# The last group's rows of the first two experts by one-hot products instead of through the expert buffer

## The reference, cut to what matters

```
Q, K, V = sign(x * bq), sign(x * bk), x * bv
x1 = layernorm(x + where(causal, sigmoid(4 * Q @ K.T / sqrt(d)), 0) @ V)
probs = softmax(x1 @ w_router);  top1 = argmax(probs);  gate = probs[top1]
pos = cumsum(onehot(top1)) - 1;  accepted = pos < C
slot = where(accepted, top1 * C + pos, E * C)
buf = zeros(E * C + 1, H).at[slot].set(x1)
y = (silu(buf @ w_gate) * (buf @ w_up)) @ w_down      # for each expert
out = layernorm(x1 + where(accepted, y[slot] * gate, 0))
```

## Time and profile before

| | us |
|---|---|
| median of 3 runs | 535.84 (534.91 to 535.91) |
| the profiled execution | 535.45 |
| its span, first to last instruction | 533.7 |
| last product of attention starts | 300.09 |
| first product of expert 0 starts | 324.26 |
| PE busy over the span | 512.2 (96%) |

### The profile page before, as it was taken

One profiled execution on the slowest core, in us unless ns is written; L12 is line 12 of the kernel. 1 busy time (PEld: TensorE's weight loads), 2 busy tenths in 40 slices (PEclk: granted clock), 3 DMA queues, 4 the chain that ended last, 5 costly groups with the idle time before them and its releaser, 6 DMA issues.

```text
span 533.7 us, 12148 instructions
## 1 busy us (share of the span) xinstructions
PE 512.2 (96%) x3983; PEld 457.7 (86%) x4021; DVE 406.8 (76%) x1033; ACT 380.5 (71%) x774; POOL 383.8 (72%) x494
## 2 busy tenths in 40 slices
PE   6999999999999999999999988999999999999992
PEld 5889899898998898998989747999998999999991
DVE  3885888886777948798766636888888888888884
ACT  5886968878868869788686513677776766777763
POOL 4647878777879688777785270577787877788876
PEclk9999999999999999999999999999999999999997
DMA  8996332263332432318841016477776666777211
GB/s 249 367 360 198 90 100 61 80 178 102 110 85 82 123 110 80 92 50 276 246 158 62 2 43 160 120 235 220 207 230 205 200 194 207 207 238 216 77 42 51
DMA packets 91919, 81.54 MB, mean 153 GB/s; under 512 B 31642, under 2 KB 83082, under 8 KB 91856
## 3 DMA queue, kind: packets, MB, share of 16 engines
q1 hardware_dynamic: 84320, 66.38, 42.0%
q0 software_dynamic: 6912, 14.30, 7.7%
q10 hardware_dynamic: 624, 0.07, 0.1%
HBM read 44.33 MB, written 37.90 MB: 154 GB/s over the span
## 4 chain that ended last, share of the span: by engine, by line
PE 90%; issue 3%; POOL 2%; DMA 2%; DVE 2%; ACT 1%; SPq 0%; POOLq 0%; DVEq 0%
PE ps L937 12%; PE ps L938 12%; PE ps L939 12%; PE ps L915 11%; PE ps L1101 8%; PE ps L1109 7%; PE ps L1102 7%; PE ps L1137 5%; PE ps L1145 3%; PE ps L1074 3%; PE ps L956 2%; PE ps L969 2%; PE ps L1134 1%; PE ps L1136 1%; PE ps L1135 1%
## 5 line engine op out<-in xcount | busy, mean ns | idle before, releaser
L937 PE MATMUL ps<-v_hl,hl_ring 128*128 128x256 f32 x544 | 178.2, 328 | 0.2 <-DVE hl_ring L1217 0.2
L938 PE MATMUL ps<-v_hl,hl_ring 128*128 128x256 f32 x544 | 153.4, 282 | 0.0
L939 PE MATMUL ps<-v_hl,hl_ring 128*128 128x256 f32 x544 | 153.2, 282 | 0.0
L937 PEld LDWEIGHTS ps<-v_hl,hl_ring 128*128 128x128 f32 x544 | 103.4, 190 | 14.8 <-issue 0.6
L1217 DVE TENSOR_TENSOR hl_ring<-ps,hl_ring 128x512 fp32r<-128x512 f32 (+3 forms) x160 | 94.0, 601 | 18.7 <-ACT ps L710 13.2
L938 PEld LDWEIGHTS ps<-v_hl,hl_ring 128*128 128x128 f32 x544 | 103.5, 190 | 2.8
L708 ACT ACTIVATE hl_ring<-ps 128x512 fp32r<-128x512 f32 (+3 forms) x160 | 86.6, 541 | 23.2 <-PE ps L915 22.8
L939 PEld LDWEIGHTS ps<-v_hl,hl_ring 128*128 128x128 f32 x544 | 103.1, 190 | 0.0
L710 ACT ACTIVATE ps<-ps 128x512 f32<-128x512 f32 (+3 forms) x160 | 87.8, 548 | 0.0
L544 POOL DMA_INDIRECT expert_rows<-xrow,slot x64 | 64.4, 1006 | 29.3 <-issue 21.3
L1101 PE MATMUL ps<-hl_ring,v_hl 128*128 128x320 f32 x256 | 80.8, 328 | 0.3 <-DVE hl_ring L1488 0.3
(11 more groups left out here) (179 smaller groups left out, 1126.4 us busy)
## 6 DMA issues: line engine op xcount, KB each, us to landing
expert_rows<-xs SPq DMA_DIRECT2D x40, 258.0 KB, 6.6
xs<-expert_rows SPq DMA_DIRECT2D x32, 258.0 KB, 2.8
out_dram<-alone SPq DMA_DIRECT2D x16, 512.0 KB, 3.2
xall<-in_L_ffn_w_gate_dram SPq DMA_DIRECT2D x32, 256.0 KB, 4.1
xall<-in_L_ffn_w_up_dram SPq DMA_DIRECT2D x32, 256.0 KB, 4.3
xall<-in_L_ffn_w_down_dram SPq DMA_DIRECT2D x32, 256.0 KB, 4.9
xall<-in_L_attn_x_dram SPq DMA_DIRECT2D x15, 512.0 KB, 5.8
xs<-expert_rows SPq DMA_DIRECT2D x31, 64.5 KB, 3.2
```

Of the source, the lines that this page charges most:

```text
L937: mm(o, ah, v_hl[:, 0, j, :], start=(j == 0 and i % 2 == 0), stop=False, skip_group_check=True)
L938: mm(o, ah, v_hl[:, 1, j, :], start=False, stop=False, skip_group_check=True)
L939: last = mm(o, al, v_hl[:, 0, j, :], start=False, stop=(j == GT * g + i), skip_group_check=True)
```

## The change

Expert 0's and expert 1's rows are put together in two parts. After the scatter of `last + 2` has landed, SP loads the rows as they then are (`base_in`), with the last group's rows still zero; PE turns them with ordinary products with the identity that leave the accumulation open (`early_rows`). Once the slots of the last group are known, DVE compares them with the numbers of the slots of each expert (`slot_of`, written by POOL after the first sequence; `slot_f`, the slots as float) and writes tables of ones and zeros (`hits_0` 4 times 128x384, `hits_1` 4 times 128x256). PE adds the last group's rows times these tables into the same PSUM banks (`last_rows`), with the rows split into a high part by ACT (`last_h`) and a low part by POOL (`last_l`). The scatter of `last + 3` still takes place, behind the `base_in` waits, and the rows of experts 0 and 1 are loaded again, since gate, token numbers and residual are read from them.

Moved besides: `place` and `gate` of `last + 2` from behind the last attention step into steps 35 to 37; three of its four scatter transfers ahead of the last group's roots and the fourth between the two halves of them (`first_root`, `second_root`); the weight splits of experts 0 and 1 into attention (on ACT two steps earlier; the low part of expert 0 on DVE in step 33, that of expert 1 on POOL); the turned rows of expert 1 ahead of the products of expert 0, so that the first two turns of the expert stage lie in another order. The 49 `keep_warm` products and the two ahead of `turn(0, 0)` are gone.

```
+            pool.wait_ge(gate_step, 3 * (last + 2) + 2)
+            pool.wait_ge(wh_ready, 2)
+            g_.tensor_tensor(w_l[:, 1, :, :], raw[:, 1, 0:WK, :], w_h[:, 1, :, :].bitcast(F32), ALU.subtract)...
+            scatter(last + 2, 0, range(GT - 1))
+            first_root(last + 3)
+            scatter(last + 2, 0, range(GT - 1, GT))
+            second_root(last + 3)
             pool.wait_ge(x1_ready, x1_by_act(last + 3, GT))
             pool.wait_ge(x1_late, GT // 2)
+            pool.wait_ge(last_high, 1)
+            g_.tensor_tensor(last_l, xrow[:, 1, :, 0:D], last_h.bitcast(F32), ALU.subtract).then_inc(last_low, 1)
             token_numbers(last + 3, 1)
+            pool.wait_ge(base_in[0], 48)
+            pool.wait_ge(base_in[1], 16)
             scatter(last + 3, 1)
...
+            def early_rows(e):
+                pe.wait_ge(base_in[e], 48 if e == 0 else 16)
+                for c in range(DC):
+                    for t in range(CT if e == 0 else CFULL):
+                        mm(turned_tile(e, t, c), xs[:, e, t, c * P:(c + 1) * P], ident[:, :],
+                           start=(t == 0 and (e == 0 or c == 0)), stop=False, skip_group_check=True)
+            def last_rows(e, hits):
+                for i in range(GT):
+                    pe.wait_ge(hit_ready, e * GT + i + 1)
+                    for rows in (last_h, last_l):
+                        for c in range(DC):
+                            o = ps[:, c, 0:W0] if e == 0 else ps[:, M1, c * W1:(c + 1) * W1]
+                            last = mm(o, rows[:, i, c * P:(c + 1) * P], hits[:, i, :], start=False,
+                                      stop=(i == GT - 1 and rows is last_l), skip_group_check=True)
+                last.then_inc(xs_turned, 1)
+            early_rows(0)
+            early_rows(1)
+            pe.wait_ge(last_high, 1)
+            pe.wait_ge(last_low, 1)
+            last_rows(0, hits_0)
+            last_rows(1, hits_1)
+            turn(0, 0, ahead=False)
+            gate_up(0, 1, 0)
+            down(0, 0)
+            turn_x(0, 2)
+            gate_up(0, 1, 1)
...
+            for hits, at, w in ((hits_0, 0, W0), (hits_1, W0, W1)):
+                for i in range(GT):
+                    v_.tensor_scalar(hits[:, i, :], slot_of[:, at:at + w], slot_f[:, i:i + 1], None, ALU.is_equal)
```

More of the change, by code:

```diff
@@ L151, in bass_postln_attn_moe_kernel @@
                     for n in range(2))
+        last_h, last_l = (r_flat[:, n * 2 * XN + XN:n * 2 * XN + XN + GT * D].rearrange("p (i d) -> p i d", d=D)
+                          for n in range(2))
+        W0, W1 = CFULL * P + P, CFULL * P
+        hits_0, hits_1 = (v_hl[:, n, 2 * WK:2 * WK + w * GT // D, :].rearrange("p k f -> p (k f)")
+                          .rearrange("p (i t) -> p i t", t=w) for n, w in enumerate((W0, W1)))
         HN = FC * CAP
@@ L233, in bass_postln_attn_moe_kernel @@
         scattered = [sem(f"scattered{i}") for i in range(2)]
+        cols_ready = sem("cols_ready")
+        slots_known = sem("slots_known")
+        hit_ready = sem("hit_ready")
+        last_high = sem("last_high")
+        last_low = sem("last_low")
+        base_in = [sem(f"base_in{i}") for i in range(2)]
         raw_in = [sem(f"raw_in{i}") for i in range(UR)]
@@ L421, in _ @@
                 store_alone(last + q, q % 2)
-            for par in range(2):
-                sp.wait_ge(scattered[par], 16 * GT * B * NG // 2)
+            sp.wait_ge(scattered[0], 16 * GT * B * NG // 2)
+            sp.wait_ge(scattered[1], 16 * GT * (B * NG // 2 - 1))
+            for e in range(2):
+                if e == 1:
+                    sp.wait_ge(x1_ready, x1_by_act(last + NG - 1, GT))
+                    sp.wait_ge(x1_late, GT // 2)
+                sp.dma_start(xs[:, e, 0:CFULL, :], buf_rows[e * CAP:e * CAP + CFULL * P, :]
+                             .rearrange("(i p) w -> p i w", p=P)).then_inc(base_in[e], 16)
+                if e == 0:
+                    for h in range(2):
+                        sp.dma_start(xs[h * CREST:(h + 1) * CREST, 0, CFULL, :],
+                                     buf_rows[h * CAP + CFULL * P:(h + 1) * CAP, :]).then_inc(base_in[0], 16)
+            sp.wait_ge(scattered[1], 16 * GT * B * NG // 2)
+            load_xs(2)
+            sp.wait_ge(xs_turned, 2)
             load_xs(0)
-            sp.dma_start(xs[CREST:2 * CREST, 0, CFULL, :], buf_rows[CAP + CFULL * P:2 * CAP, :]).then_inc(rest_in[0], 16)
+            load_rest(1)
+            store_alone(last + NG - 1, (NG - 1) % 2)
+            load_xs(3)
             load_xs(1)
[L427 to L430, removed]
+            load_ids(0)
+            load_rest(0)
+            load_ids(1)
             load_rest(2)
             load_rest(3)
-            for e in range(U):
+            for e in range(2, U):
                 load_ids(e)
@@ L537, in token_numbers, with scatter @@
                 atleast(pool, tok_step, G * 2 + 2, settle=True)
-            def scatter(G, par):
+            def scatter(G, par, tiles=range(GT)):
                 atleast(pool, gate_ready, G + 1, settle=True)
                 atleast(pool, slot_ready, G + 1, settle=True)
-                for i in range(GT):
+                for i in tiles:
                     g_.indirect_dma_start(
@@ L750, in batch @@
                     weights(b, k)
+                    if last and k == NS - 6:
+                        act.wait_ge(pv_done, (B - 1) * NS + OFF[3] + WK)
+                        high_weights(0, 0)
                     for g in (3, 0, 1, 2):
@@ L776, in batch @@
                             values_high(bb, q)
[L777 removed]
+                    if last and k == NS - 4:
                         act.wait_ge(pv_done, (B - 1) * NS + OFF[3] + 2 * WK)
[L780 removed]
+                        high_weights(0, 1)
             for tiles, landed, done in ((slice(0, GT // 2), x_half, sgn_half), (slice(GT // 2, GT), x_in[0], sgn_ready)):
@@ L800, in _ @@
             copy_x1t(B * NG - 1, range(1))
+            act.wait_ge(x1_late, GT // 2)
+            s_.activation(last_h, xrow[:, 1, :, 0:D], ACT.Copy).then_inc(last_high, 1)
             copy_lgt(B * NG - 1)
@@ L855, in turn @@
                 silu(R, n, 0)
-                if ahead:
+                if ahead and R * U + n >= 1:
                     high_x(R, n + 1)
@@ L1047, in _ @@
             pe.wait_ge(al_ready, B * NS)
-            keep_warm(22)
+            keep_warm(22, bank=3)
             pe.wait_ge(slot_ready, G)
@@ L1060, in _ @@
             turn_logits(G)
-            keep_warm(6)
+            keep_warm(6, bank=3)
             counts(G)
-            keep_warm(49)
             def turn_x(R, n):
@@ L1315, in place_and_gate @@
                 dve.wait_ge(route_step, base + 3)
+                v_.scalar_tensor_tensor(out=slot_f[:, :], in0=rt[:, 0, :], scalar=E * CAP - 1.0, in1=over,
+                                        op0=ALU.add, op1=ALU.add).then_inc(slots_known, 1)
                 v_.scalar_tensor_tensor(out=slot[:, par, :], in0=rt[:, 0, :], scalar=E * CAP - 1.0, in1=over,
@@ L1349, in batch @@
                             row_statistics((b - 1) * NG + g, 0, g % 2)
+                    if last and k == NS - 7:
+                        low_weights(0, 0)
                     for g in (3, 0, 1, 2):
@@ L1357, in batch @@
                             pick(G, k - PICK[g])
-                        late = last and g == NG - 2
-                        if k == PLACE[g] and not late:
+                        early = last and g == NG - 2
+                        if k == (PLACE_LAST if early else PLACE[g]):
                             place(G, g % 2)
                         for part in range(2):
-                            if k == GATE[g][part] and not (late and part == 1):
+                            if k == (GATE_LAST if early else GATE[g])[part]:
                                 gate(G, g % 2, part)
```

50 lines of the change are left out of this document (30 added, 20 removed).

## The result

The changed kernel takes 539.66 us (median of six runs, 539.23 to 540.54) where the kernel before takes 535.44: a ratio of 1.0083, 95% interval 1.0073 to 1.0093. It is slower by 4.2 us. The forecast was 530.3 us, faster by 5.5. The profiled executions span 537.8 and 533.7 us.

The account below looks back on a forecast made before the run. The handover's chain of scatter transfers, loads and split was taken to bound the kernel, PE elsewhere. The first product at 319.2 instead of 324.70 gives 5.5 us: 535.45 - 5.5 = 529.95, plus 0.39, 530.3 us; range 528.4 to 532.8.

Parts of the forecast that it names:

- The handover: Stretch from attention's end to expert 0's first product, bound by scatter and loads, not PE; shortening it gains 5.5 us.
- Step 1: Three scatter transfers of the group ahead on POOL, done by 302.6, covered until the statistics at 302.67; cost 0.
- Step 2: Fourth scatter transfer of the group ahead starts at 305.52, lands at 307.81; SP issues the first load at 307.87.
- Step 3: SP's early loads of expert 0's and expert 1's rows, complete at 312.3.
- Step 4: PE ahead of expert 0: `early_rows` 2.15 us, `last_rows` 4.7 us, from 312.3 to 319.2.
- S: Start of expert 0's first product on PE: forecast 319.2, against 324.26 before; gain is 324.70 - S.
- Steps 5 and 6: Work beside PE (tables, splits, slot numbers) hidden; last group's scatter lets expert 2's rests land at 325.0, needed at 326.7.
- the common point: Start of expert 1's `gate_up(0, 1, 1)`, 332.46 before, S + 7.76 changed; behind it both kernels go through the same order.
- Clock: PE idles 1.4 us ahead of `early_rows` without `keep_warm`; clock might fall: chance 0.04 slower (537.2 us), 0.05 short fall.
- The fourth rival: Experts' stage has its own pace (rows, weights or token numbers arriving), PE waits there for the gain; within 0.2%, chance 0.04.

Follow-up runs that it names:

- after_pad8: The changed kernel with 8 instructions of already satisfied waits added on POOL ahead of its first turn of the expert stage: 529.2 us, 0.9889 of the kernel before.
- before_pad8: The kernel before with 8 instructions of already satisfied waits added on POOL ahead of its first turn of the expert stage: 545.1 us, 1.0185.
- lag1: after_pad8 with one useless memset on POOL, once, behind its first store, a delay of 0.66 us: 529.42 us, ratio 0.9891.
- lag2: after_pad8 with two useless memsets on POOL, once, behind its first store, a delay of 1.34 us: 539.23 us, ratio 1.0071.
- after_pad2: The changed kernel with 2 instructions of already satisfied waits added on POOL ahead of its first turn of the expert stage: 539.19 us, 1.0069.
- after_split_low: The changed kernel with DVE's low_weights of experts 2 and up in two pieces of 512 and 768 columns: 529.26 us, 0.9884 of the kernel before.
- after_silu_first: The changed kernel with ACT's second silu of an expert moved ahead of second_norm of the expert two back: 536.44 us, 1.002.
- before_pad8_split: before_pad8 with DVE's low_weights of experts 2 and up in two pieces: 535.38 us, 1.0005 of the kernel before.

## Why the prediction was wrong

The handover, which was the whole sum, held:

- *Step 1.* The three transfers start at 298.56, 299.85 and 301.12 (forecast 298.8, 300.1, 301.4); the cover held.
- *Step 2.* Fourth transfer 305.37, landed 307.85, SP 307.87 (305.52, 307.81, 307.87).
- *Step 3.* The loads are complete at 311.46 (312.3): the last took 2.62 us, at the fast end of the rows.
- *Step 4.* `early_rows` 2.50 us (2.15; ten f32 products of 128 columns take 0.25 each), `last_rows` 4.69 (4.7). S = 318.69 (319.2): the loads are 0.84 us early, `early_rows` 0.35 longer, and S is 0.5 early.
- *Steps 5 and 6.* No wait for a table in the chain, none for expert 2's rests. From S to the common point 7.5 us (7.76): before, the first product of expert 0 stands in the chain with 0.38 us, now with 0.15.
- *Clock.* The granted clock is 1.00 in every stretch from 310.9 to 326.2, and PE's pause ahead of `early_rows` was 0.42 us instead of 1.4. The rule that was weighed there (the Trainium skill, TensorE: Matmul & The Clock Gate, "Part 1: The HAM clock gate") was not put to a test by it: no run here shows the clock of this stretch fall.

The gain at the common point was thus 6.3 us where 5.5 was forecast, and after_pad8, which keeps all of the change, comes out at 529.2: 6.0 us under the 535.18 of before in that comparison. Had nothing followed, the forecast would have been 1 us too slow. Much the same gain stands between kernels of the same pace: 6.0 us in step, 6.1 with the pieces in both (535.38 to 529.26), and 5.4 with the hole in both (before_pad8's 545.1 to 539.66). So the sign of the result does not come from the handover: the kernel before had the luck that its first store did not lie at the place of the hole, and the change moved it there.

**The step that failed** is the common point: "behind them both kernels go through the same order", and with it "a microsecond taken out of the handover is one off the time, as long as no new wait takes its place". The order is the same; the pace is not a property of the order alone. The fourth rival, "the experts' stage has a pace of its own", named the place but not the mechanism. I gave it 0.04 because the chain before is all products behind 324.26, and I priced it as a gain that is only lost, not as a second, slower pace. A chain that is all PE says that PE ends last; it doesn't say by how much. The other circle had 0.66 to 1.34 us of slack in the first turn (lag1 and lag2; the 1.2 of after_pad2 tips it too) and, once late, lies only 0.55 us a pair above PE. And the part on the change counted the cost of POOL's added instructions as work (the tables' numbers, the last rows), not as places in its program: eight more of them ahead of the first store made it the 453rd.

The account, from the `silu` rows of ACT, the kernel after and then after_pad8:

```profile
336.65 0.44 ACT L898 ACTIVATE a_buf<-ps 128x320 f32<-128x320 f32 x1 [0.16 <-PE ps L1176]
342.02 0.42 ACT L898 ACTIVATE a_buf<-ps 128x320 f32<-128x320 f32 x1
...
499.52 0.42 ACT L898 ACTIVATE a_buf<-ps 128x320 f32<-128x320 f32 x1
```
```profile
337.19 0.44 ACT L900 ACTIVATE a_buf<-ps 128x320 f32<-128x320 f32 x1 [0.16 <-PE ps L1178]
341.17 0.44 ACT L900 ACTIVATE a_buf<-ps 128x320 f32<-128x320 f32 x1
...
491.07 0.44 ACT L900 ACTIVATE a_buf<-ps 128x320 f32<-128x320 f32 x1
```

The kernel after is 0.54 us ahead at the first row, 0.85 behind at the second (this turn, with the hole, costs 1.39) and 8.45 behind at the third, twelve pairs later: eleven at 13.05 and one at 14.01 make 7.6 more than twelve at 12.49. The last 1.25 come behind them, to spans of 537.8 and 528.1. The one pair of 14.01 (460.91 to 474.92) is in every late kernel at the same pair, with a store that starts 0.7 us later than its neighbours. In the kernel after the next store, at 468.05, thereby falls into `low_weights` (from 467.92) and lasts 2.20 us instead of 0.97. What holds the first of them back is open.

## What to carry to other kernels

Before a gain ahead of a steady loop is booked, ask how much slack the loop's second-longest circle has: one useless operation of a known length, put once on an engine that is off the path, measures it, as here on POOL. A change that adds instructions to an engine moves everything behind them in its program, and eight waits that do nothing were worth 10 us here, either way; so a difference within 2% is worth measuring again with a few harmless instructions more. And where a long operation of one engine holds up another's small ones, it is worth trying in two pieces.

## What was not expected of the hardware

**Waiting for code.** In six kernels the first store starts 1.9 to 2.1 us behind the start of the 8 KB packet: 335.4 and 337.33 (the kernel after), 333.8 and 335.75 (after_pad2), 340.4 and 342.31 (before_pad8), 333.7 and 335.63 (after_split_low), 337.6 and 339.51 (after_silu_first), 339.9 and 342.00 (before_pad8_split). Where it came while the last scatter ran (316.7 in after_pad8), nobody waited for it. The Trainium skill (Runtime: NRT & Kernel Launch, "Instruction fetch mechanics") calls the cost of such a crossing "mostly hidden", since the sequencer brings the next page while it executes the current one. If the holes are such crossings, they were exposed here by 1.2 to 2.9 us, and the packets have 8 KB, where the page has blocks of 16 KiB. Beside a later packet of the same queue, at 413.3 in the kernel after, POOL shows no hole. Why the one at the first store comes so late wasn't settled.

**POOL stands behind DVE.** A POOL operation of 0.2 to 0.9 us that starts during a DVE operation of 1.48 us with two inputs in SBUF lasts at least until that one is done (2.03, 1.19, 1.47 us above), and a store of 1.11 lasts 2.10. The Trainium skill (SBUF — State Buffer, "SBUF: two separate sides") describes the shared pair of ports as an exclusive lock for a whole instruction, given to whichever starts first; the rows agree, and the two pieces of after_split_low, 884/2023/2035 to 722/805/1304, show that POOL gets its turn between two instructions of DVE.
